# A second PSUM bank for Gram products and transposed features, taken from a shared ring of four

## The reference

```
for i in range(6):                       # on layer-normed x
    x = x + mamba2(rmsnorm(x), t_*[i])   # scan along time, 128 steps, for each band
    x = x + mamba2(rmsnorm(x), b_*[i])   # scan along bands, 16 steps, for each time
x = x_in + x
out = x + moe(layernorm(x))              # 16 experts, 64 -> 128 -> 64, top 2
```

## Time and profile before

| | |
|---|---|
| Median of 3 runs | 1553.57 us |
| Profiled execution, its own time | 1553.12 us |
| Span of that execution in the trace | 1551.4 us |
| PE busy | 1220.9 us (79%) |
| DVE busy | 909.3 us (59%) |
| ACT busy | 720.8 us (46%) |
| First g of block 0, first g of block 1 | 71.32 us, 118.78 us |
| First g of block 23 | 1238.46 us |

### The profile page before, as it was taken

One profiled execution on the slowest core, in us unless ns is written; L12 is line 12 of the kernel. 1 busy time (PEld: TensorE's weight loads), 2 busy tenths in 40 slices (PEclk: granted clock), 3 DMA queues, 4 the chain that ended last, 5 costly groups with the idle time before them and its releaser, 6 DMA issues. The chain is left out here.

```text
span 1551.4 us, 47280 instructions
## 1 busy us (share of the span) xinstructions
PE 1220.9 (79%) x20280; PEld 635.6 (41%) x20280; DVE 909.3 (59%) x1667; ACT 720.8 (46%) x1358; POOL 276.1 (18%) x406
## 2 busy tenths in 40 slices
PE   0688688688686886878868868778688962999998
PEld 0254344344343453434434434444344442333332
DVE  4276455565464565644745546546465576777776
ACT  1356455454364554645645536455456531333332
POOL 8011211221121112211212112112211151000000
PEclk8799899899898997998979979989899985999999
DMA  3010001100011000101001010001100022000000
GB/s 68 7 20 6 22 8 23 29 10 21 6 22 33 9 8 16 22 23 20 5 22 20 15 26 10 21 9 21 32 10 9 8 42 30 1 7 1 8 8 7
DMA packets 69600, 26.45 MB, mean 17 GB/s; under 512 B 54928, under 2 KB 66320, under 8 KB 69392
## 3 DMA queue, kind: packets, MB, share of 16 engines
q1 hardware_dynamic: 69392, 23.42, 7.5%
HBM read 9.96 MB, written 1.05 MB: 7 GB/s over the span
## 5 line engine op out<-in xcount | busy, mean ns | idle before, releaser
L1249 DVE TENSOR_TENSOR em<-em,gx 128x1536 f32<-128x1536 f32 (+1 forms) x192 | 283.7, 1478 | 134.4 <-ACT em L972 134.4
L972 ACT ACTIVATE em<-ring 128x512 f32<-128x512 f32 x480 | 255.1, 599 | 207.4 <-PE ring L725 207.2
L550 POOL TENSOR_TENSOR ysq<-yg 128x256 f32<-128x256 f32 x192 | 117.6, 612 | 900.5 <-DVE yg L1267 900.5
L725 PE MATMUL ring<-rt,lt 128*64 128x512 bf16 x960 | 152.9, 416 | 61.6 <-ACT em L972 45.5
L742 PE MATMUL ybank<-em,xdt 64*32 64x64 f32 (+1 forms) x12288 | 189.9, 244 | 0.9 <-issue 0.6
L742 PEld LDWEIGHTS ybank<-em,xdt 64*32 64x32 f32 x12288 | 157.6, 108 | 36.0 <-issue 35.2
L708 PE MATMUL gx<-cm,bc 16*64 16x128 f32 (+1 forms) x768 | 75.9, 275 | 81.8 <-DVE em L1249 79.7
L1105 ACT ACTIVATE em<-ring 128x512 f32<-128x512 f32 x128 | 69.5, 595 | 148.4 <-PE ring L862 148.4
L619 PE MATMUL ring<-xsq,mean 128*128 128x512 f32 x96 | 65.8, 775 | 89.9 <-ACT xsq L933 69.4
L991 ACT ACTIVATE xs<-ring,col 128x512 f32<-128x512 f32 x96 | 60.7, 683 | 147.8 <-PE ring L667 147.8
L1275 DVE TENSOR_TENSOR on<-oss,rr 128x256 f32<-128x256 f32 x96 | 40.2, 419 | 133.0 <-ACT rr L982 132.9
(11 more groups left out here) (168 smaller groups left out, 1692.4 us busy)
## 6 DMA issues: line engine op xcount, KB each, us to landing
x_b<-x_t SPq DMA_DIRECT2D x48, 128.0 KB, 3.0
rt<-lt SPq DMA_DIRECT2D x240, 12.0 KB
cm<-bc SPq DMA_DIRECT2D x96, 32.0 KB, 2.0
cw<-in_L_conv_t_cw SPq DMA_DIRECT2D x6, 320.0 KB
cw<-in_L_conv_b_cw SPq DMA_DIRECT2D x6, 320.0 KB
x_in<-in_x SPq DMA_DIRECT2D x4, 256.0 KB, 4.3
xs<-in_L_ffn_w SPq DMA_DIRECT2D x2, 512.0 KB, 7.1
zs<-in_L_ffn_w SPq DMA_DIRECT2D x2, 512.0 KB, 9.2
```

Of the source, the lines that this page charges most:

```text
L550: pool.tensor_tensor(out=ysq[u][:, i % 2, :], in0=yg[u][:, i % 2, :], in1=yg[u][:, i % 2, :], op=ALU.mult).then_inc(s_ysq, 1)
L725: mm = pe.matmul(o[HALF * ab:HALF * (ab + 1), :].rearrange("p (h t) -> p h t", h=HEADS), lt[:, n % 2, ab, i, :], rt[i // 4][:, blk, :, i % ...
L972: emptied(act.activation(em[:, p % EM_SLOTS, :, HALF * j:HALF * (j + 1)], o.rearrange("p (h t) -> p h t", h=HEADS), ACT.Exp), "seg", n, i, ...
L1249: dve.tensor_tensor(e, e, gx[:, 0:wide].rearrange("p (o t) -> p o t", o=1).to_broadcast([P, HEADS, wide]), ALU.mult).then_inc(s_w, 1)
```

## The change

`gx` becomes two banks, `gx0` and `gx1`, used by the pair's parity. g(p) waits for weigh(p-2) where it waited for weigh(p-1). `weigh` and `x_dt` read the pair's own bank. The ring has three banks where it had four. No engine's order of instructions changes, nor does what any instruction computes; only the banks, and with them the waits.

```diff
-RING = 4
+RING = 3
...
-        gx = ctx.enter_context(nc.psum_tensor("gx", [P, CK], F32))
+        gxs = [ctx.enter_context(nc.psum_tensor(f"gx{u}", [P, CK], F32)) for u in range(2)]
...
-        bank = ring + [gx, ybank[:, 0, :], ybank[:, 1, :], oss]
+        bank = ring + gxs + [ybank[:, 0, :], ybank[:, 1, :], oss]
...
     # g_and_xt (PE)
-                if p:
-                    pe.wait_ge(s_w, p)
+                if p >= 2:
+                    pe.wait_ge(s_w, p - 1)
+                gx = gxs[p % 2]
...
     # x_dt and weigh (DVE)
+                gx = gxs[p % 2]
```

## The result

The changed kernel takes **1619.15 us** (median of 4 runs, 1613.39 to 1626.12) against 1553.49 us: the ratio is 1.0409, 95% interval 1.0367 to 1.0451. I had forecast 1584 us with a range of 1562 to 1603. The direction was right, the size was not: +65.7 us where I had +31.

A forecast was written before the change was run, and what follows sets the result against it. No engine is full; a chain from engine to engine bounds the kernel. -37.8 + 63.2 - 13.2 + 10.9 + 6.3 + 1.7 = +31.1 us on 1553.12 gave 1584 us, range 1562 to 1603.

The forecast's parts named there:

- the gain at g: Pairs: g(i+1) runs while PE would wait, so mix(i) starts when weigh(i) ends; 37.8 us saved.
- 10.9 + 6.3: Kind 0 blocks: both means and turn_dt wait for ring reads; 10.9 us in seven blocks, 6.3 in five with the stall.
- 1.2 us of relief: Ahead of kind 0 blocks: PE's wait for rt transfers takes in 1.2 us of delay at eleven boundaries, -13.2 us.
- the second rival: Gain and price cancel: boundary price 1.3 to 1.8 us in place of 2.8; 1540 to 1569 us, chance 0.12.
- The boundary: Between blocks: four ring requests wait for later reads, 2.8 us behind kind 1, 2.7 behind kind 0; 63.2 us in all.
- The start: First block: project_bc and project_x(0, 1) are delayed by ring reads, and rt transfers pass it on; 1.7 us.
- The weights' stall: ACT's ten waits for the next pass's weights, 134.1 us in all: length left alone by the change.
- turn_dt starts behind a read: Sign in kind 0: turn_dt starts behind the first read of exps(6); its delay priced at 0.5 us.
- the mixture of experts: Its eight banks come in the same order as before: no change in time.
- The third: Early g(i+1) is of no use, so only the prices stand, 69 us: 1622 us, chance 0.07.
- The fourth: New PE gaps of 0.5 to 0.9 us in the boundary lower the granted clock; a tenth gives 1622 us, chance 0.03.
- my two signs of being wrong: In the boundary: PE's new waits don't move ACT, or the granted clock is under 1.00.

The follow-up runs named there:

- nobody reading ybank: gate_y reads an SBUF stand-in for ybank and mix drops that wait: 1554.64 us on the kernel before, 1589.79 us on the changed kernel.
- the ring alone: Kernel before with three ring banks in place of four, one gx bank as before, eighth bank unused: 1635.85 us, ratio 1.0531.
- ybank read earlier: Changed kernel with gate_y(4) moved ahead of bias_dt on DVE, so ahead of weigh(5): 1610.42 us, ratio 1.0358.

## Why the prediction was wrong

**The step that failed: "mix(i) starts at the end of `weigh(i)`", in the gain at g.** Every term of the gain of 37.8 us hangs on that sentence. mix(i) has two waits, `weighed` and `y_bank_read`, and I priced one. The second was in the code, in `mix_states`, and its producer stands behind weigh(i) in DVE's order; its 0.60 us are in the trace of the kernel before, at 764.45. There it ended last only once, for 0.3 us, since g came between, and so the view of waits has just that one short row for it. The gain at a wait was not the length of what leaves it but the distance to the next releaser: 0.91 to 0.66 us in kind 0.

**How much it was.** For the pairs my sum had -37.8 + 10.9 + 6.3 - 13.2 = -33.8 us, of which about -31 belongs to blocks 1 to 22, the stretches that I measured; they came out at +1.9. With nobody reading ybank they came out at -32.4 us by the same measure. That this is so near is in part luck. Against the ring alone (+7.5) it is a gain of 39.9 us, where I had 33.6 for these blocks, and the ring alone should have given about +2.4. So both the gain and the price were some 5 to 6 us too low, and cancel. One term I misread: I took 1.2 us of relief from the 14.0 us in 12 waits for `rt`, but one of these, 2.98 us, is in block 0. The eleven others are 11.0 us in sum, so they could not give 13.2; in the changed kernel all eleven are gone. One sum is wrong and nothing else uses it: in the second rival, 1.0 to 1.5 us less in 23 boundaries are 23 to 34 us, not 9 to 23.

**What held.** The boundary, with some luck: 63.2 us forecast, 65.1 measured, but the measured sum holds several us of slow clock, which I had not put in. In a boundary at full clock 720.33 to 735.69 became 761.19 to 779.08, 2.53 us more in kind 0 (2.7 forecast), and 2.7 in kind 1 (2.8 forecast), which makes some 60 us. The start: project_x(0, 1) begins 3.49 us behind ACT's first read of x where it began 1.78 behind it, 1.7 us more, as forecast:

```profile
62.26 1.27 ACT L992 ACTIVATE xs<-ring,col 128x512 f32<-128x512 f32 x2 [5.36 <-PE ring L667]
...
65.75 3.70 PE L667 MATMUL ring<-h_t,wt 64*128 64x512 f32 x16 [0.69 <-ACT bc L1014]
```

The weights' stall was unchanged. In kind 0 turn_dt starts behind a read, with 0.41 us idle, and the mean too (0.56 us on average). From ACT's last table load to the end, which is the mixture of experts but for its beginning, the two kernels took 251.8 and 251.2 us.

**The rivals.** The third, that the gain goes nowhere, gave 1622 us and is nearest to the result, for another reason than I named: PE does reach g early, but mix is then held by DVE's read of `ybank`, of which the rival says nothing. That its number fits so well is luck too: the 69 us in it are 13 too low for the ring, and the second bank gives a part of that back. I gave it 0.07. The fourth, the falling clock, is true in a small part; a clock under 1.00 in the boundary was one of my two signs of being wrong. In the earlier trace rows the clock fell behind a long stall. In the changed kernel it also falls within boundaries, or just ahead of one, for some 3 to 6 us at a time:

```profile
370.00:373.00 3.00, 2.52 (x47) 1.17 (x32) 2.87 (x4) 1.88 (x4) 0.40 (x1) 0.56 0.00 0
373.00:376.00 3.00, 3.00 (x10) 1.24 (x8) 0.00 (x0) 0.98 (x1) 0.00 (x0) 0.50 0.00 0
376.00:379.00 3.00, 2.85 (x12) 1.12 (x8) 0.12 (x1) 0.47 (x1) 0.00 (x0) 0.80 0.00 0
...
824.00:827.00 3.00, 1.85 (x14) 0.80 (x12) 0.75 (x2) 1.54 (x3) 0.00 (x0) 1.00 0.04 12
827.00:830.00 3.00, 2.23 (x6) 0.65 (x8) 0.00 (x0) 1.53 (x4) 0.00 (x0) 0.62 0.06 16
```

In the first of these, project_x took 6.10 us where it takes 3.71. Two such project_x and three halves of project_z (1.79 to 1.97 us for 1.13) stand in the changed kernel's trace, one project_x and no project_z in that of before, four halves and three project_x in that of the ring alone, and none in those of the two kernels with four ring banks and two for gx. The other traces have two halves (nobody reads ybank, changed kernel), four halves (ybank read earlier, changed kernel), and one, two and one project_x (the three further kernels with four ring banks and one gx bank). In the changed kernel each costs 0.7 to 2.4 us itself, 6.3 us in sum. Its averages of the boundary lie 0.38 and 0.19 us over a boundary at full clock (17.90 and 17.61), 6.7 us in all, which is the same size. All 13 slow halves of project_z are in the four traces with three ring banks, each behind the new wait of 0.74 us, and none is in the six with four. That speaks for the new waits as the cause there, but it was not tested by itself, and slow project_x stand in four of the traces with four ring banks too.

## What to carry to other kernels

Before a wait is taken away, list every wait of the instruction that is to start earlier, and ask for each when its producer runs; one that is hidden today has hardly a row in a list of waits, here 0.3 us for what became 71.9. The gain is the distance from the wait's end to the next releaser's, here 0.25 us and not 0.85. A bank taken from a shared ring can be priced from the rows by asking, for each request, which read it now follows: 69 us summed here, 82 measured. Better than taking it there was to let the ring serve a rarely used bank, which cost nothing here.

## What the runs showed of the hardware

The granted clock fell not only behind the stall of nearly 10 us. It was 0.56 and 0.50 in the changed kernel at 370 to 376 us, behind a wait of 1.45 us for yt, one of 12 waits of that length in this trace, and stayed at 1.2 GHz for some time although PE was busy. At 827 us it was 0.62 behind waits of 0.88 and 0.74 us. The same waits in most other boundaries left it at 1.00, so from these runs I can't say which will do it. I had held that gaps of this size are harmless because one gap of 1.69 us was the earlier trace rows; one gap was too few to say so.
